# Softmax denominators inverted in a compact tile filled and spread by transfers; the upper output half written by ScalarE

## The reference

```python
qkv = x @ Wqkv.T
q, k, v = map(merge_heads, jnp.split(qkv, 3, axis=-1))      # 16 heads of 32
dots = jnp.einsum('bhid,bhjd->bhij', q, k) * dh ** -0.5
dots = jnp.where(causal_mask, -jnp.inf, dots)
attn = jax.nn.softmax(dots, axis=-1)
out = jnp.einsum('bhij,bhjd->bhid', attn, v)                 # then @ Wout.T + bout, + x, norm
```

## Time and profile before

| | us |
|---|---|
| median of 3 runs | 2791.89 (2785.82 to 2792.28) |
| the profiled execution's own time | 2788.14 |
| its span, first to last instruction | 2786.3 |
| PE busy, DVE busy, ACT busy, POOL busy | 2563.3, 1913.3, 1102.4, 782.0 |
| reciprocals (L767), x128 | 116.5 |
| sums on POOL (L623), x88 and x24 | 398.2 and 108.8 |
| mean granted TensorE clock | 0.957 |

### The profile page before, as it was taken

One profiled execution on the slowest core, in us unless ns is written; L12 is line 12 of the kernel. 1 busy time (PEld: TensorE's weight loads), 2 busy tenths in 40 slices (PEclk: granted clock), 3 DMA queues, 4 the chain that ended last, 5 costly groups with the idle time before them and its releaser, 6 DMA issues. The chain is left out here.

```text
span 2786.3 us, 44691 instructions
## 1 busy us (share of the span) xinstructions
PE 2563.3 (92%) x15124; PEld 1064.3 (38%) x15124; DVE 1913.3 (69%) x3125; ACT 1102.4 (40%) x2002; POOL 782.0 (28%) x276
## 2 busy tenths in 40 slices
PE   8999699998999899999998679999999999999998
PEld 3444223232232233332322335454544544454543
DVE  5442787877778677778882557776867676767764
ACT  4231155555555455555555223231323323232320
POOL 0000254553636344445455211111201011111100
PEclk9999799999999999999999889999999999999999
DMA  7953500302020302012001210101010101001000
GB/s 245 306 193 140 122 9 6 73 6 70 9 69 9 69 6 55 23 34 74 5 12 56 86 43 1 58 1 59 1 43 16 43 16 43 16 1 58 1 16 16
DMA packets 115902, 146.74 MB, mean 53 GB/s; under 512 B 9086, under 2 KB 87678, under 8 KB 114653
## 3 DMA queue, kind: packets, MB, share of 16 engines
q1 hardware_dynamic: 115677, 143.77, 16.9%
HBM read 91.57 MB, written 51.91 MB: 51 GB/s over the span
## 5 line engine op out<-in xcount | busy, mean ns | idle before, releaser
L715 ACT ACTIVATE probs<-st_ps 128x512 f32<-128x512 f32 (+3 forms) x1280 | 628.2, 533 | 590.5 <-PE st_ps L821 294.6
L746 DVE TENSOR_REDUCE seg_max<-s_ps 128x1 f32<-128x512 f32 (+3 forms) x1280 | 699.8, 599 | 230.3 <-PE s_ps L804 136.9
L804 PE MATMUL s_ps<-k_pair,q_pair 96*128 96x512 f16 (+3 forms) x1280 | 438.7, 364 | 70.0 <-DVE seg_max L746 56.4
L821 PE MATMUL st_ps<-q_pair,k_pair 98*128 98x512 f16 (+3 forms) x1280 | 434.6, 360 | 26.6 <-issue 19.5
L623 POOL TENSOR_TENSOR total<-total,probs 128x2048 f32<-128x2048 f32 x88 | 398.2, 4525 | 62.1 <-ACT probs L715 59.6
L841 PE MATMUL o_ps<-probs,v_sb 128*32 128x512 f32 (+3 forms) x2560 | 321.4, 572 | 0.7 <-issue 0.7
L1381 PE MATMUL fps<-x2T,w_p_hi 128*128 128x512 f16 x1024 | 317.2, 379 | 0.0
L1381 PE MATMUL fps<-w_p_hi,hT 128*128 128x512 f16 x1024 | 306.0, 381 | 0.0
L821 PEld LDWEIGHTS st_ps<-q_pair,k_pair 98*128 98x128 f16 x1280 | 117.5, 98 | 374.4 <-ACT probs L715 287.4
L804 PEld LDWEIGHTS s_ps<-k_pair,q_pair 96*128 96x128 f16 x1280 | 125.6, 99 | 276.9 <-DVE seg_max L746 191.3
L1343 DVE SCALAR_TENSOR_TENSOR x<-fps,gates_un,x 128x512 f32<-128x512 f32 x256 | 184.0, 746 | 36.0 <-PE fps L1381 33.4
(11 more groups left out here) (162 smaller groups left out, 3553.7 us busy)
## 6 DMA issues: line engine op xcount, KB each, us to landing
k_pair<-k_parts SPq DMA_DIRECT2D x96, 128.0 KB, 5.0
q_pair<-q_parts SPq DMA_DIRECT2D x96, 128.0 KB, 5.6
x_raw<-xT_in SPq DMA_DIRECT2D x8, 1024.0 KB, 6.5
q_parts<-qk_out SPq DMA_DIRECT2D x32, 256.0 KB, 3.6
k_parts<-qk_out SPq DMA_DIRECT2D x32, 256.0 KB, 4.0
piece_raw<-w_in SPq DMA_DIRECT2D x8, 1024.0 KB, 8.7
v_rows<-v_out SPq DMA_DIRECT2D x32, 256.0 KB, 2.1
w_parts<-piece_cut SPq DMA_DIRECT2D x8, 1024.0 KB, 5.6
```

The costliest lines, as they stand in the source:

```text
L715: nc.scalar.activation(probs[:, k % NP, h, off:], st_ps[:, p % (2 * NVU) % RING, off:], ACT.Exp, scale=SCALE).then_inc(exp_done.sem, 1)
L746: nc.vector.reduce_max(seg_max[:, h, j, s:s + 1], s_ps[:, slot, 0:width], AX.X).then_inc(s_read.sem, 1)
L804: last = nc.tensor.matmul(s_ps[:, slot, 0:width], q_pair[a][0:NR, h, q0:q0 + P], k_pair[a][0:NR, h, s * CH:s * CH + width], start=True, st ...
L821: last = nc.tensor.matmul(st_ps[:, slot, off:], k_pair[a][:, h, kt * P:(kt + 1) * P], q_pair[a][:, h, c * CH + off:(c + 1) * CH], start=Tr ...
```

## The change

`den` and `o_raw` get two slots. The four reciprocals of the whole `den` go. In their place SP moves one row of each head (4 rows of 512) into a tile of 128x16, DVE inverts that, SP stores it to a buffer in memory (`inv_rows`), and reads it back in four transfers, one a head, each spread over 32 rows. POOL multiplies with the result. The cast to the upper half goes from DVE to ACT. The lags, and the DVE time that `schedule()` keeps free, change with it; the lags come to 8 (DEN_MOVED), 14 (INVERTED), 15 (INV_STORED), 19 (INV_LOADED), 23 (SCALED), 27 (STORED) and 28 (TAIL).

```diff
     TAKEN = VALUES + 1, SUMS + 1
-    RECIPS = [SUMS + 3 + 2 * n for n in range(PIECES)]
-    SCALED = RECIPS[-1] + 1
+    DEN_MOVED = TAKEN[1] + 1
+    INVERTED = DEN_MOVED + 6
+    INV_STORED = INVERTED + 1
+    INV_LOADED = INV_STORED + 4
+    SCALED = INV_LOADED + 4
     STORED = SCALED + 4
     TAIL = STORED + 1
...
         for t in LAST_TILE:
-            for lag in RECIPS:
-                busy[(t * HG + HG - 1 + lag) % NVU] += 0.85
+            busy[(t * HG + HG - 1 + INVERTED) % NVU] += 0.2
...
-        o_raw = sb("o_raw", [P, CH], F32)
-        den = sb("den", [P, CH], F32)
+        o_raw = sb("o_raw", [P, 2, CH], F32)
+        den = sb("den", [P, 2, CH], F32)
+        inv_small = sb("inv_small", [P, 2, CH // DH], F32)
+        inv = sb("inv", [P, 2, CH], F32)
...
 # POOL
                 c = chunk_at(s, SCALED, first, end)
                 if c is not None:
-                    pool.wait_ge(recips.sem, recips.at(i, c * PIECES + PIECES - 1))
+                    pool.wait_ge(inv_loaded, 16 * HG * (2 * CPB * i + c + 1))
                     pool.wait_ge(split_done.sem, split_done.at(i, c - 1))
-                    nc.gpsimd.tensor_tensor(o_sb[:], o_raw[:], den[:], ALU.mult).then_inc(scaled.sem, 1)
+                    nc.gpsimd.tensor_tensor(o_sb[:], o_raw[:, c % 2], inv[:, c % 2],
+                                            ALU.mult).then_inc(scaled.sem, 1)
...
 # SP, behind the loads for the group after the next and ahead of the store
+                c = chunk_at(s, DEN_MOVED, first, end)
+                if c is not None:
+                    sp.wait_ge(den_taken.sem, den_taken.at(i, c))
+                    sp.dma_start(inv_small[:, c % 2], den[0:P:DH, c % 2]).then_inc(den_moved, 16)
+                c = chunk_at(s, INV_STORED, first, end)
+                if c is not None:
+                    sp.wait_ge(recips.sem, recips.at(i, c))
+                    sp.dma_start(inv_rows[c % 2].rearrange("h (a b) -> (h a) b", b=CH // DH),
+                                 inv_small[:, c % 2]).then_inc(inv_stored, 16)
+                c = chunk_at(s, INV_LOADED, first, end)
+                if c is not None:
+                    sp.wait_ge(inv_stored, 16 * (2 * CPB * i + c + 1))
+                    for h in range(HG):
+                        sp.dma_start(inv[h * DH:(h + 1) * DH, c % 2], inv_rows[c % 2, h].partition_broadcast(
+                            DH)).then_inc(inv_loaded, 16)
...
 # ACT
-                    act.wait_ge(scaled.sem, scaled.at(i, c - 1))
-                    nc.scalar.activation(o_raw[:], o_ps[:], ACT.Copy).then_inc(o_taken.sem, 1)
+                    act.wait_ge(scaled.sem, scaled.at(i, c - 2))
+                    nc.scalar.activation(o_raw[:, c % 2], o_ps[:], ACT.Copy).then_inc(o_taken.sem, 1)
...
+                c = chunk_at(s, SCALED + 2, first, end)
+                if c is not None:
+                    act.wait_ge(scaled.sem, scaled.at(i, c))
+                    act.wait_ge(o_stored[c % 2], stored_at(CPB * i + c // 2))
+                    nc.scalar.activation(o_out[:, c % 2, 0], o_sb[:], ACT.Copy).then_inc(o_hi_done.sem, 1)
...
 # DVE
-                for n, lag in enumerate(RECIPS):
-                    c = chunk_at(s, lag, first, end)
-                    if c is not None:
-                        if n == 0:
-                            dve.wait_ge(den_taken.sem, den_taken.at(i, c))
-                        piece = den[:, n * CH // PIECES:(n + 1) * CH // PIECES]
-                        nc.vector.reciprocal(piece, piece).then_inc(recips.sem, 1)
-                c = chunk_at(s, SCALED + 2, first, end)
+                c = chunk_at(s, INVERTED, first, end)
                 if c is not None:
-                    dve.wait_ge(scaled.sem, scaled.at(i, c))
-                    dve.wait_ge(o_stored[c % 2], stored_at(CPB * i + c // 2))
-                    nc.vector.tensor_copy(o_out[:, c % 2, 0], o_sb[:]).then_inc(o_hi_done.sem, 1)
+                    dve.wait_ge(den_moved, 16 * (2 * CPB * i + c + 1))
+                    nc.vector.reciprocal(inv_small[:, c % 2], inv_small[:, c % 2]).then_inc(recips.sem, 1)
```

More of the change, by code:

```diff
@@ L399, in _, with self_attention @@
                     last.then_inc(prod_ready, 1)
-def self_attention(nc, S, x_rows, q_parts, k_parts, v_rows, o_parts):
+def self_attention(nc, S, x_rows, q_parts, k_parts, v_rows, o_parts, inv_rows):
     NR = 3 * DH
@@ L429, in self_attention @@
     RING = 3
-    PIECES = 4
     VALUES, SUMS = 4, 6
     TAKEN = VALUES + 1, SUMS + 1
-    RECIPS = [SUMS + 3 + 2 * n for n in range(PIECES)]
-    SCALED = RECIPS[-1] + 1
+    DEN_MOVED = TAKEN[1] + 1
[3 more added lines that the diff above has]
+    SCALED = INV_LOADED + 4
     STORED = SCALED + 4
@@ L565, in self_attention @@
         rows_moved = sems(nc, stack, "rows_moved", 2)
+        den_moved, inv_stored, inv_loaded = (stack.enter_context(nc.semaphore(s)) for s in
+                                             ("den_moved", "inv_stored", "inv_loaded"))
         st_ready = Count(nc, stack, "st_ready", 2 * NVU)
@@ L576, in self_attention @@
         steps = Count(nc, stack, "steps", 2 * 2 * CPB)
-        recips = Count(nc, stack, "recips", 2 * CPB * PIECES)
+        recips = Count(nc, stack, "recips", 2 * CPB)
         scaled = Count(nc, stack, "scaled", 2 * CPB)
@@ L702, in _ @@
             den_taken.lead(act)
+            o_hi_done.lead(act)
             def step(i, s, first, end):
@@ L724, in step @@
                     act.wait_ge(pv_done.sem, pv_done.at(i, c // CPB * NKU + LAST_TILE[c % CPB]))
-                    nc.scalar.activation(den[:], den_ps[:], ACT.Copy, scale=1.0 / XS).then_inc(den_taken.sem, 1)
+                    nc.scalar.activation(den[:, c % 2], den_ps[:], ACT.Copy, scale=1.0 / XS).then_inc(den_taken.sem, 1)
+                c = chunk_at(s, SCALED + 2, first, end)
[3 more added lines that the diff above has]
+                    nc.scalar.activation(o_out[:, c % 2, 0], o_sb[:], ACT.Copy).then_inc(o_hi_done.sem, 1)
             laps(act, step)
@@ L730, in _ @@
         def _(dve):
-            for count in (s_read, max_ready, steps, recips, o_hi_done):
+            for count in (s_read, max_ready, steps, recips):
                 count.lead(dve)
@@ L1476, in layer @@
     v_rows = dram("v_rows", [N, D], F32)
+    inv_rows = dram("inv_rows", [2, HG, CH], F32)
     w_parts = dram("w_parts", [2 * KT, P, 2, KT * D], F16)
@@ L1484, in layer @@
                 q_parts, k_parts, v_rows, w_parts, k_blocks, v_ctx)
-        self_attention(nc, S, x_rows, q_parts, k_parts, v_rows, o_parts)
+        self_attention(nc, S, x_rows, q_parts, k_parts, v_rows, o_parts, inv_rows)
         second_half(nc, S, x_rows, o_parts, mask, w_parts, k_blocks, v_ctx, out)
```

## The result

The changed kernel takes 2922.8 us (median of 4 runs, 2918.26 to 2931.11) against 2790.5 before on the same chip: ratio 1.048, 95% interval 1.0453 to 1.0508. The forecast had the sign and less than half of the size: +56 against +132 us. The profiled execution took 2923.49 us, its span 2921.6, mean granted clock 0.932 (before 0.957).

The account below looks back on a forecast made before the run. PE was taken as the bound, losing time where it waits for DVE. From the profiled 2788.1 us: - 73 - 3 + 8 + 117 + 7 = 2844, given as 2846 us against the median; range 2780 to 2884.

Parts of the forecast that it names:

- What bounds it, and the casts: Attention: PE is the bound and waits for DVE; 23 stalls behind casts held by POOL additions go, 73 us gained.
- The group's end: Small transfer queues behind 25 loads; PE idles 16 us in six places, plus 3.5 us low clock each: +117 us.
- ACT's wait for POOL: Chunk ends: ACT waits some 2 us for POOL's product; 0.5 us on each of 16 ends, +8 us (0 to 32).
- The tail: Behind the last unit: three serial transfers and a small reciprocal replace the reciprocals; +7 us (3 to 12).
- The reciprocals become small: DVE in each chunk: 3.7 us become 0.1 to 0.5; PE gains 3 us (0 to 12), the rest already hidden.
- The sign by group 7: Group 7, without the group-start idle time, should be 9 us shorter; if no shorter, casts did not cause the stalls.
- The rival that relief of DVE reaches PE: Attention: less DVE work also closes PE's small gaps, 56 us more gained, 2778 us; chance of this side 0.13.

Follow-up runs that it names:

- e4: Kernel before, with only the cast to the upper half moved from DVE to ACT; 2722.9 us.
- e1: Changed kernel, with schedule() keeping free the DVE time of the kernel before, so AUX units and units "rows" stand where they stood; 2851.4 us.
- e11: Changed kernel with the old DVE times in schedule(), and the 25 loads spread over 22 steps with the small transfers in between; 2770.6 us.
- e8: Kernel before with the cast on ACT, no reciprocals (outputs not the layer's), and the change's line in schedule(); 2765.3 us.
- e7: Kernel before with the cast on ACT and no reciprocals, so outputs are not the layer's; 2709.0 us.
- e10: Changed kernel, new plan kept, high half of max_parts made by ACT, low half replaced by a DVE reduction of zeros; 2818.0 us.
- e12: Changed kernel, new plan, high half of max_parts by ACT, low half replaced by a reduction of zeros, loads spread over 22 steps; 2728.1 us.

## Why the prediction was right and wrong

- *What bounds it, and the casts*: right. 73 us forecast, 64 measured (e4).
- *The group's end*: right in place, order and size of the idle time: 16 us in six places, 94 of PE's 97.2 us. By `schedule()` units 0 to 17 bring four AUX units more than before and not three; PE stopped 14.5 us into group 1, where 14.2 were forecast. The price was right too, as far as the runs can tell. e1 and e4 have the same plan and the cast on ACT, and their groups 1 to 6 took 968.7 and 851.9 us:

```profile
470.09:1438.78 968.69, 834.40 (x5953) 276.31 (x5951) 583.10 (x1080) 499.51 (x1033) 437.55 (x132) 0.92 0.17 43
```

```profile
467.99:1319.89 851.90, 816.52 (x5953) 274.06 (x5951) 650.06 (x1152) 500.36 (x1032) 436.97 (x132) 0.97 0.17 41
```

That is 117 us where 117 were forecast (other, smaller differences between the two are in it). Mending it gives back less, 81 us in e11 against e1, since PE's waits for exponentials grow by 27 us there.
- *ACT's wait for POOL*: +8 forecast. ACT waits 1.5 to 2.1 us at 15 of the 16 ends, as forecast, and PE's waits for exponentials are 20.2 us where they were 6.4: 14 us of idle time, 7 of it at two places, of 4.1 and 2.9 us. No run parts its price from the rest.
- *The tail*: +7 forecast, +3.7 measured, since the small transfers take 1.4 to 2.1 us and not the 2.6 of a 256 KB store.
- *"The reciprocals become small"*: here it failed. The step put "AUX units being spread more evenly" into a gain of 3 us (0 to 12). The moved plan is a loss of 56 us in e8 against e7 and of 71 in e1, and the hold behind it is worth 105 (e10), which takes in the waits of this kind that the old plan has too. I had the hold in the earlier trace rows, and a moved plan in the diff, and did not ask which other instructions of that kind the plan would move under POOL's additions. L752 was too small to be among my rows: 14.3 us in all, mean 461 ns where its minimum is 174. That gap was the sign. Neither my bounds nor a rival held this, so even the range ended 39 us short.
- *The sign by group 7*: it "should be 9 us shorter", and if it was no shorter, the casts were not the cause. It was 7.3 us longer, and the casts were the cause all the same: in e4 it took 117.5 us, 8 less than before. In the kernel after, a wait of 5.1 us for max_parts and one of 4.1 us for ACT stand in it. A sign that the rest of the change can turn over tells nothing of one part.
- *The rival that relief of DVE reaches PE*: e7 bounds it at 14 us. Its 126 us a group rest on no row; group 1 took 136 to 139 us in e4, e7 and e12.

The terms close. The cast is -64 (e4). Transfers, ACT's wait, the tail and the relief together are e1 against e4, measured on one chip: +129, and the forecast had 117 + 8 + 7 - 3 = 129; that its parts are off by a few us each and their sum is not, is in part luck. The plan is +71. That makes +136, against +132 measured; the forecast lacked the 71, and had the cast 9 too high.

## What to carry to other kernels

When a schedule is planned from costs, a changed cost can move every other instruction: list those that can be held by another engine, whatever their size, and see what they would now stand beside. A small transfer issued behind a burst waited for the burst's issues (7 us) and its data (9 us); before putting one on a path that an in-order engine waits for, look at what is issued ahead of it. Split a combined change: here one half, the cast on ScalarE, was worth -64 us, and the other lost some 200.

## What the runs showed of the hardware that I had not expected

A DVE instruction of 174 ns on 16 columns was held for 4.45 us, as long as POOL's whole addition; an instruction with two SBUF inputs was held as well (median 2821 ns), a reduction in the same place never (222 ns at most), and an ACT copy beside the additions neither (632 ns at most). And the low clock follows each of the six long idle times: the granted clock is 0.50 over the 5 us behind each, here from 504.75, right after PE's 15.76 us of waiting:

```profile
504.75:509.75 5.00, 5.00 (x26) 1.46 (x27) 3.71 (x6) 2.17 (x4) 0.84 (x1) 0.50 0.20 54
```
